# Expert down products as three 256-column matmuls in one half bank, in place of a 512-column matmul with a right half that ScalarE and GpSimd finish

## The reference, cut to what matters

```python
# x: (16, 128, 256); proj_in: (8, 512, 256), proj_out: (8, 256, 512)
x = _layernorm(x + attention(x))
h = relu(einsum('edi,bsi->bsed', proj_in, x))
o = einsum('eid,bsed->bsei', proj_out, h)
gate = einsum('bks,kse->bse', ctx_512, one_hot(itok, 8))
x = _layernorm(x + einsum('bsei,bse->bsi', o, gate))
x = _layernorm(x + ffn(x))
```

## Time and profile before

| | us |
|---|---|
| median of 3 runs | 773.61 |
| lowest and highest | 773.35, 773.98 |
| the profiled execution | 772.94 |
| its span, first to last instruction | 771.0 |
| TensorE busy | 750.3 |
| VectorE busy | 605.3 |
| ScalarE busy | 430.2 |
| GpSimd busy | 272.9 |
| experts' stage, about | 104 to 455 |

### The profile page before, as it was taken

How to read it: one execution, slowest core, us unless ns; L and a number is a source line. 1 busy time by engine, 2 the same in 40 slices (tenths; PEclk the granted TensorE clock), 3 DMA queues, 4 the chain that set the end, 5 groups by cost and what they waited for, 6 DMA issues and landing times.

```text
span 771.0 us, 11852 instructions
## 1 busy us (share of the span) xinstructions
PE 750.3 (97%) x3699; PEld 632.6 (82%) x3699; DVE 605.3 (79%) x1294; ACT 430.2 (56%) x839; POOL 272.9 (35%) x293
## 2 busy tenths in 40 slices
PE   9999999999999999999999999899899998999995
PEld 7788988888888888888888887688787986887885
DVE  5789989876798989999676667967966569778566
ACT  6788743434555656555443346465677454646672
POOL 2777243225574747557252330301200203111003
PEclk9999999999999999999999999999999999999999
DMA  7800000004345445351731021144363101363201
GB/s 269 291 1 0 2 1 1 1 22 141 119 130 206 151 144 183 99 197 39 260 115 44 13 69 20 56 136 164 110 191 112 53 1 55 110 219 124 95 1 58
DMA packets 31706, 77.15 MB, mean 100 GB/s; under 512 B 8736, under 2 KB 13472, under 8 KB 27808
## 3 DMA queue, kind: packets, MB, share of 16 engines
q1 hardware_dynamic: 31360, 76.18, 29.4%
q10 hardware_dynamic: 288, 0.26, 0.1%
HBM read 58.08 MB, written 16.78 MB: 97 GB/s over the span
## 4 chain that ended last, share of the span: by engine, by line
PE 75%; DVE 14%; ACT 5%; issue 4%; POOL 1%; DVEq 0%; POOLq 0%; ACTq 0%
PE bank L1365 15%; PE bank L1249 8%; PE bank L1343 7%; PE bank L1344 7%; PE bank L1348 7%; PE bank L1513 6%; PE bank L1514 6%; PE bank L1364 6%; PE bank L1221 5%; DVE part_r L2012 3%; ACT hring L1135 3%; DVE part_f L2024 2%; DVE part_f L2031 2%; PE bank L1368 2%; DVE part_f L2103 2%
## 5 line engine op out<-in xcount | busy, mean ns | idle before, releaser
L1365 PE MATMUL bank<-wx_both,hx_hi 128*128 128x512 f32 x512 | 191.4, 397 | 0.0
L1513 PE MATMUL bank<-hring,wring 128*128 128x512 f32 x448 | 176.9, 395 | 8.0 <-DVE part_r L2012 5.9
L1514 PE MATMUL bank<-part_r,wring 128*128 128x512 f32 x448 | 175.8, 392 | 0.0
L992 ACT ACTIVATE hx_hi<-bank 128x512 fp32r<-128x512 f32 x128 | 76.5, 599 | 175.1 <-PE bank L1348 173.9
L710 POOL TENSOR_TENSOR x_tok<-right,x_tok 128x256 f32<-128x256 f32 x128 | 95.0, 743 | 173.3 <-ACT right L999 170.0
L2012 DVE TENSOR_TENSOR part_r<-part_f,hring 128x512 fp32r<-128x512 f32 x144 | 95.4, 687 | 51.6 <-ACT hring L1135 51.4
L1785 DVE SCALAR_TENSOR_TENSOR hx_lo<-bank,hx_hi 128x512 fp32r<-128x512 f32 x128 | 87.9, 687 | 51.4 <-ACT hx_hi L992 49.9
L1365 PEld LDWEIGHTS bank<-wx_both,hx_hi 128*128 128x128 f32 x512 | 96.0, 188 | 16.7
L1364 PE MATMUL bank<-wx_both,hx_lo 128*128 128x256 f32 x384 | 108.7, 283 | 0.0
L1513 PEld LDWEIGHTS bank<-hring,wring 128*128 128x128 f32 x448 | 85.2, 190 | 28.5 <-DVE part_r L2012 7.9
L1514 PEld LDWEIGHTS bank<-part_r,wring 128*128 128x128 f32 x448 | 85.3, 190 | 17.6
(11 more groups left out here) (204 smaller groups left out, 1431.7 us busy)
## 6 DMA issues: line engine op xcount, KB each, us to landing
wring<-h_dram SPq DMA_DIRECT2D x28, 1024.0 KB, 4.8
wx_raw<-in_wx SPq DMA_DIRECT2D x16, 512.0 KB, 7.9
raw_quads<-in_wffn SPq DMA_DIRECT2D x16, 512.0 KB, 5.7
h_dram<-sums SPq DMA_DIRECT2D x8, 1024.0 KB, 4.4
h_dram<-raw_quads SPq DMA_DIRECT2D x8, 512.0 KB, 6.5
stage<-in_wffn SPq DMA_DIRECT2D x12, 256.0 KB, 2.6
x_tok<-in_x SPq DMA_DIRECT2D x1, 2048.0 KB, 11.0
h_dram<-raw_quads SPq DMA_DIRECT2D x8, 256.0 KB, 6.7
```

The costliest lines, as they stand in the source:

```text
L992: act.activation(hx_hi[:, place, c], bank[b][:, :], ACT.Relu).then_inc(s_relu_ok, 1)
L1365: mm = pe.matmul(DBANK[j][:, :].rearrange("p (h d) -> p h d", h=2), hx_hi[:, place, c, a], wo_hl[:, :, c], start=(c == 0), stop=(c == XC - 1))
L1513: pe.matmul(into[:, :], w, b_hi[:, k], start=(k == 0 and i in (0, 1, 3)), stop=False, skip_group_check=True)
L1514: mm = pe.matmul(into[:, :], w, b_lo[:, k], start=False, stop=(k == KH - 1), skip_group_check=True)
```

## The change

In `down` each chunk now has three matmuls of 256 columns, all into the left half of the bank: `hx_hi` with the high weights, `hx_hi` with the low weights, `hx_lo` with the high weights. The hardware's accumulation makes the sum. ScalarE's `right_half`, GpSimd's `right_added`, their two semaphores and all waits on them go. Where VectorE waited for GpSimd's row it now waits for its own. `gated` is as before, but completes the row.

```diff
             def down(unit, place, e, j, expert):
                 wo_h = wx_hi[:, e, OUT].rearrange("p (c d) -> p c d", c=XC)
-                wo_hl = wx_both[:, :, e, OUT].rearrange("p h (c d) -> p h c d", c=XC)
+                wo_l = wx_lo[:, e, OUT].rearrange("p (c d) -> p c d", c=XC)
                 ...
                 pe.wait_ge(s_gated_ok, unit * J + j + 1)
-                pe.wait_ge(s_right_ok, unit * J + j + 1)
                 a = slice(j * S, j * S + S)
                 for c in range(XC):
                     if j == 0:
                         pe.wait_ge(s_hlo_ok, unit * XC + c + 1 + 2)
-                    if c > 0:
-                        pe.matmul(DBANK[j][:, 0:D], hx_lo[:, place, c, a], wo_h[:, c], start=False, stop=False)
-                    mm = pe.matmul(DBANK[j][:, :].rearrange("p (h d) -> p h d", h=2), hx_hi[:, place, c, a], wo_hl[:, :, c],
-                                   start=(c == 0), stop=(c == XC - 1))
-                    if c == 0:
-                        pe.matmul(DBANK[j][:, 0:D], hx_lo[:, place, c, a], wo_h[:, c], start=False, stop=False)
+                    for h, w, last in ((hx_hi, wo_h, False), (hx_hi, wo_l, False), (hx_lo, wo_h, c == XC - 1)):
+                        mm = pe.matmul(DBANK[j][:, 0:D], h[:, place, c, a], w[:, c], start=(c == 0 and h is hx_hi and w is wo_h), stop=last)
                 mm.then_inc(s_down_mm, 1)
...
-            def right_added(unit, g, j):
-                pool.wait_ge(s_right_ok, unit * J + j + 5)
-                row = x_tok[:, g * J + j]
-                pool.tensor_tensor(row, right[:, j % 2], row, ALU.add).then_inc(s_row_ok, 1)
...
-            def right_half(unit, g, j, expert):
-                act.wait_ge(s_gated_ok, unit * J + j + 5)
-                act.wait_ge(s_row_ok, unit * J + j + 3)
-                gate = gates[:, bass.ds(g * J + j, 1), bass.ds(expert, 1)].rearrange("p b e -> p (b e)")
-                act.activation(right[:, j % 2], DBANK[j][:, D:2 * D], ACT.Copy, scale=gate).then_inc(s_right_ok, 1)
...
                 def gated(unit, g, j, expert):
                     dve.wait_ge(s_down_mm, unit * J + j + 1 + 2 * J)
                     dve.wait_ge(s_gated_ok, unit * J + j + 1)
-                    dve.wait_ge(s_row_ok, unit * J + j + 1 + J - back)
```

More of the change, by code:

```diff
@@ L97, in decoder_kernel @@
         o_right = base[0]
-        right = small("right", [2, D])
+        small("y_wide_at", [2, D])
         assert base[0] <= 229344
@@ L256, in decoder_kernel @@
         s_gated_ok = sem("gated_ok")
-        s_right_ok = sem("right_ok")
-        s_row_ok = sem("row_ok")
         s_wxhi_ok = sem("wxhi_ok")
@@ L732, in step @@
             def step(g, further, last):
[L733 to L742, removed]
+                if last:
+                    expert_low(0, 2)
+                if further:
+                    root(g + 2)
             root(1)
@@ L762, in pair @@
                     for j in range(J):
-                        right_added(p * 8 + u, u % G, j)
                         if u == 1:
@@ L1003, in step @@
                     relu(g * 2 + 1, 1, c, c % 2)
-                    if c > 0:
-                        right_half(g * 2, g, c - 1, 0)
-                    elif g > 0:
-                        right_half(g * 2 - 1, g - 1, J - 1, 1)
                     if c == 2 and front:
@@ L1013, in step @@
                     relu(g * 2 + 2, 0, c, c % 2)
[L1014 to L1017, removed]
                     if c == 1 and not front:
                         expert_high(0, 2, (2, 3))
-            act.sem_inc(s_right_ok, 4)
             halves_x(0)
@@ L1058, in pair @@
                             keep(0)
[L1060 to L1063, removed]
                         if u == 1:
@@ L1070, in _ @@
             pairs_of_experts(act, pair)
-            right_half(E * G - 1, G - 1, J - 1, E - 1)
             act.wait_ge(s_wide_f, 1)
@@ L1439, in ffn_wide @@
                         pe.wait_ge(s_gated_ok, B * E + 4)
-                        pe.wait_ge(s_right_ok, B * E + 4)
                     if m == 2:
@@ L1710, in _ @@
             dve.sem_inc(s_gated_ok, 4)
-            dve.sem_inc(s_row_ok, 4)
             dve.sem_inc(s_stage_used, 2)
@@ L1786, in low, with gated @@
                                              op0=ALU.max, op1=ALU.subtract).then_inc(s_hlo_ok, 1)
-                def gated(unit, g, j, expert, back=J):
+                def gated(unit, g, j, expert):
                     dve.wait_ge(s_down_mm, unit * J + j + 1 + 2 * J)
                     dve.wait_ge(s_gated_ok, unit * J + j + 1)
-                    dve.wait_ge(s_row_ok, unit * J + j + 1 + J - back)
                     gate = gates[:, bass.ds(g * J + j, 1), bass.ds(expert, 1)].rearrange("p b e -> p (b e)")
@@ L1881, in pair @@
                                 norm2_low(0)
-                            gated(p * 8 + u, u % G, c, p * 2 + u // G, B)
+                            gated(p * 8 + u, u % G, c, p * 2 + u // G)
                             if u == 6 and c == 2 and last:
@@ L1900, in pair @@
                             dve.tensor_reduce(wide_col[:, :], neq[:, :], AX_X, ALU.max).then_inc(s_wide_c, 1)
-                            dve.wait_ge(s_row_ok, (p * 8 + 5) * J + 4)
+                            dve.wait_ge(s_gated_ok, (p * 8 + 5) * J + 4)
                             norm2_stats(0)
                         if u == 6 and last:
-                            dve.wait_ge(s_row_ok, (p * 8 + 6) * J + 4)
+                            dve.wait_ge(s_gated_ok, (p * 8 + 6) * J + 4)
                             norm2_stats(J)
@@ L1910, in rest @@
                 dve.wait_ge(s_gated_ok, B * E + 4)
-                dve.wait_ge(s_row_ok, B * E + 4)
                 dve.wait_ge(s_wide_f, 1)
```

1 line of the change is left out of this document (removed).

## The result

The changed kernel takes 778.67 us (four runs, 777.87 to 779.19) against 773.50 for the kernel before (four runs). The ratio is 1.006, 95% interval 1.0047 to 1.0073, so 3.6 to 5.6 us (0.5 to 0.7%) slower; +3.2 us was forecast, to 776.8. The profiled execution has a span of 777.1 us, 6.1 more than before.

What follows compares the result with a forecast made beforehand. The prediction took TensorE's matmuls to bound the experts' stage. +3.8 us for 128 dearer tiles and -0.6 us at the crossing make +3.2, from 773.61 to 776.8 us (chance 0.60), range 773.9 to 780.2.

Steps and rivals of the forecast that it cites:

- What bounds the kernel: Experts' stage: the matmuls carry the chain of waits; ScalarE or GpSimd time counts only where it makes TensorE wait.
- The fixed price of a matmul: TensorE: each matmul costs 0.013 us beside its columns at any width; four more cost 0.053 us a tile.
- The 2.5 ns a matmul: Trainium skill's price beside the columns: four more matmuls 0.010 us a tile, 1.3 us in all; the prediction didn't adopt it.
- The alternation of widths: Old tile in the experts' stage: mixing 512 and 256 columns costs 0.02 us, saved in the new tile, leaving +0.03.
- A whole cycle, 1.41 and 1.39, makes 2.80: Tile plus up block: a short run starts early, the long matmuls behind pay back; the same total as 1.44 and 1.36.
- the third rival: Experts' stage: tile 1.44 and up block 1.39 us, a step 0.06 us longer, 780.7 us; chance 0.13.
- The crossing, -0.6 us: Crossing to the feed-forward part: VectorE normalises 1.9 us earlier without GpSimd's additions, of which 0.6 us reaches TensorE.
- the link that was to hold the rest: Crossing: the seventh chunk's gate activation on ScalarE, at 468.52 us behind its matmuls, can't move; 0.6 of 1.9 us arrives.
- The first: Experts' stage: new tile no dearer, 1.41 us, up block 1.36; 773.0 us, no measurable change; chance 0.14.
- the second: Experts' stage: short matmuls at 0.11 us, twelve of 0.115 making 1.38 us a tile; -3.8 us, 769.2 us; chance 0.05.
- The fourth: Feed-forward part: one clock halving fails to come, returning 1.5 us, 775.3 us; both, 773.8; chance 0.08.

Runs made afterwards that it cites:

- run 1: Changed kernel with the eight old matmuls a tile back, ScalarE's scaling and GpSimd's addition still gone (right half left out of the result): 772.73 us, ratio 0.9982.
- run 5: Changed kernel with the up matmuls halved too, so a step is 24 matmuls of 256 columns: 785.49 us beside 773.06.
- run 6: Kernel before without the matmuls that multiply hx_lo with the high weights (left out of the result), a step being ten 512-column matmuls: 725.86 us.
- run 7: Changed kernel with each matmul of the tile halved to 128 columns, 24 a tile, each with its own weight load: 940.5 us.
- run 4: Kernel before with the eight matmuls of tiles 1 to 3 of each unit reordered, four of 512 columns, then four of 256: 773.91 us, ratio 0.9998.
- run 3: Kernel before with chunks 0 and 1 of each tile as three 256-column matmuls, chunks 2 and 3 unchanged: 777.92 us, ratio 1.0054.
- run 2: Kernel before with twelve 256-column matmuls a tile, low-weight product to the right half, ScalarE and GpSimd finishing as before: 781.07 us, ratio 1.0087.
- run 9: Kernel before with only the last of the 32 units in the new form, without scaling or addition there: 773.09 us, ratio 0.9986.
- run 8: Changed kernel with a chunk's three matmuls ordered so that no two in a row load the same stationary block: 779.30 us.

## Why the prediction was right, and which size was off

**What bounds the kernel.** Right. The chain stayed on the matmuls, and run 1 shows that ScalarE and GpSimd relieved are worth nothing in the stage.

**The fixed price of a matmul, 0.013 us beside its columns.** Right for these two widths, and shown by uniform steps: 0.1200 us at 256 columns (run 5), 0.2267 at 512 (run 6). It isn't the price at every width (run 7). Four more of them are 0.053 us a step and, as it came out, that is the whole loss: 2.820 - 2.767. The 2.5 ns a matmul of the Trainium skill ("TensorE: Matmul & The Clock Gate", "Wait — 56ns, not 53.3ns?") are not what this kernel shows at either width.

**"The alternation of widths seems to cost 0.02 us, and the new tile has none inside."** This is the step that failed, in size. The sum took +0.03 us a tile, 3.8 us; measured were +0.053, 6.8 us. The old step is 0.020 us dearer than 14 matmuls at the fixed price (2.767 against 2.747), and I booked that as lost with the alternation. But the new step is just as much above its own price (2.820 against 2.800): it still mixes 512 and 256 columns. Run 4 shows that fewer changes of width within a step don't lower this, and in runs 5 and 6, where all widths are equal, it is gone.

| kernel | matmuls a step | at the fixed price | tile | up block | step |
|---|---|---|---|---|---|
| before | 14 | 2.747 | 1.407 | 1.360 | 2.767 |
| grouped (run 4) | 14 | 2.747 | 1.386 | 1.381 | 2.767 |
| half the chunks (run 3) | 16 | 2.773 | 1.409 | 1.397 | 2.807 |
| changed | 18 | 2.800 | 1.432 | 1.388 | 2.820 |
| all 256 (run 5) | 24 | 2.880 | 1.440 | 1.440 | 2.880 |
| all 512 (run 6) | 10 | 2.267 | 0.907 | 1.360 | 2.267 |

The fixed price is the columns at 2.4 GHz plus 0.0133 us for each matmul. Run 4's means take in the first tile of each unit, which kept the old order; run 6's are medians.

**"A whole cycle, 1.41 and 1.39, makes 2.80."** Half right. The short matmuls' early start is paid back behind the run, as run 4 shows most plainly. But the tile I read as 1.41 in the attention's output product was 1.43 here, so the cycle was 2.82. In the stage the third rival ("dearer": 0.06 us a step, tile 1.44 and up block 1.39) was nearer to the 0.053 measured (1.43 and 1.39) than the forecast's 0.03. With 0.053 the sum is 773.61 + 6.8 - 0.6 = 779.8. The two profiled executions bear that out, 772.94 and 778.92 us with spans 6.1 apart. The median of 778.67 is 1.1 below the sum and so nearer to the forecast than the mechanism was, and so far it is luck. The three executions without a trace have a granted clock of 0.995 or 0.996 and the profiled one 0.992, so they may have had one stretch at half clock less; as one of the three took 779.19 us, this stays open. The range's upper end, 780.2, was also drawn below the third rival's own 780.7, though the text says that it takes in nearly all of that case.

**The crossing, -0.6 us.** Right in mechanism and size: 0.65 us in the trace. VectorE starts 0.87 us behind its last row sum, not 0.6, and the link that was to hold the rest held it. The seventh chunk's gate activation starts as much later as the stage ends (475.13 against 468.52), and the rounding that stood 1.22 us behind it stands 0.58 us behind it now. Run 2 doesn't have it, and runs 1 and 9 do.

**The rivals.** The first (no dearer, 2.77) and the second (0.11 us a matmul within a short run, 2.74) are excluded by the step. The fourth, a halving of the clock that fails to come, didn't happen in the profiled execution: both stretches are there. It happened in run 1 and run 5 (one stretch in place of two), and run 2 has one more. So the number of stretches differed between kernels with nearly the same feed-forward part, and nothing here shows what decides it. One stretch less was worth 0.7 us (run 1) and 0.9 us (run 5) by the end, where the prediction had 1.5: TensorE loses 1.1 to 1.6 us in each, and later waits give a part back.

**Left open.** What the 0.02 us of a mixed step is. It doesn't follow the number of changes of width (two in a cycle of run 4, six in the old one, the same step), nor the length of the short run (run 4 and the changed kernel), nor the bank's half that is written (run 2), nor the neighbours (run 1), nor the order of the weights (run 8), and run 3 has 0.034. The records show it on up to five 512-column matmuls behind a 256-column one. Open too is what sets the 0.112 us of run 7.

## What to carry to other kernels

Where TensorE is the bound, count matmuls as well as columns: here each cost 0.013 us beside its columns at 256 and 512 columns, and work taken off idle engines paid for none of it. Price a changed block by the whole cycle of TensorE from one occurrence to the next, since a block's own length can shift onto its neighbour. And look for the one place where the relieved engines are waited for: the new form in the last unit alone shortened that wait by as much, at 0.2 us of dearer tiles, though a gain of the whole kernel was not shown. When differences are below 2 us, compare executions that have the same number of stretches at half clock.

## What the runs showed of the hardware

- A 256-column fp32r matmul with its own weight load goes every 0.1200 us in a uniform stream, a 512-column one every 0.2267, and 128-column ones in a run every 0.112: from 256 to 128 columns the time hardly falls.
- Behind a run of 256-column matmuls, of four or of twelve, the next six 512-column ones take 0.028 us more in all than their uniform pace (run 4 and the changed kernel), so that an untouched block reads 0.03 us longer.
- A matmul of 512 columns whose moving operand is two blocks of 256 apart costs the same as one in a single block (0.90 us for four, run 6).
- A VectorE instruction on 128x512 took 1.57 us in the median (1.62 in run 2) while ScalarE scaled and GpSimd added rows beside it, and 0.68 us without this work (changed kernel and run 1). Which of the two engines slows it no run here separates.
- The profiled executions had one (run 1), two (before, changed) or three (run 2) stretches of 3.4 us at half clock (1.2 GHz) in the middle of the feed-forward part. The further one cost 1.6 us on the spot (run 2); one less was worth 0.7 us by the end (run 1).
